# One attention layer reordered: rotary and shared-key head groups take turns

## The chip, the cores and the metric

The kernel runs on one core of one Trainium2 chip. The metric is the time of one execution in microseconds (us); lower is better. Three runs of the kernel before took 1016.63 to 1022.61 us, with a median of 1020.66.

The engines: PE multiplies matrices and writes to PSUM banks; DVE (vector) and ACT (activation) read those banks; POOL (GpSimd) works on SBUF only; SP issues all transfers (DMA).

## The reference, cut to what matters

The program is four transformer layers on 1024 tokens of width 256. Only layer 0 changes. It has two attentions on the same normalised input, added together: one of 16 heads with low-rank queries and keys and a rotary part of 64 rows per head (called MLA below), and one of 16 heads whose key and value are selected per token by a router (called shared below).

```python
    def _L0_attn_ref(x, Wqd, Wqu, Wqr, Wkvd, Wku, Wvu, Wkr, Wo):
        ...
        H, LAT, RD = (16, 64, 64)
        ...
        ql = x @ Wqd
        q = (ql @ Wqu)...
        qr = (ql @ Wqr)...
        qr = _apply_rope(qr, cos, sin)
        ckv = x @ Wkvd
        ...
        kr = _apply_rope((x @ Wkr)[:, None], cos, sin)[:, 0]
        scores = (jnp.einsum('bhtd,bhsd->bhts', q, k) + jnp.einsum('bhtd,bsd->bhts', qr, kr)) * scale
        ... # causal softmax, times v
    def _L0_ffn_ref(x, W_gate, W_qkv):
        ...
        k_shared = jnp.einsum('bth,bthd->btd', indicator, k)
        v_shared = jnp.einsum('bth,bthd->btd', gating_top1, v)
        att = jnp.einsum('bhqd,bkd->bhqk', q, k_shared) * (1.0 / math.sqrt(hd))
        ... # causal softmax, times v_shared
```

## The kernel before

Every engine runs its own program, written out by hand; semaphores tie them. The 16 heads of each attention are cut into groups of four (GH = 4). Layer 0 has eight groups: groups 0 to 3 are MLA, groups 4 to 7 are shared.

A group is worked off in eight steps kt, one per tile of 128 keys. In a step PE writes the transposed scores of the four heads into psA (L1549, L1550), ACT takes the exponential into Pr (L834, L839), POOL zeroes what the causal mask forbids (L709, `mask_exponentials`), and PE multiplies the exponentials of the step before by the values (L1587). An MLA score takes two f32 matmuls (128 rows of Kr2 and Qr2, 113 rows of Kr and Qr), a shared score one bf16 matmul. Since the scores stand transposed, the row maxima have to be known before the group starts. They come from 43 bf16 products per group (L1532, with masks L1534) into psD, which DVE reduces (L1088, 43 instructions). They are computed beside the group ahead: `max_window` and `beside` (L56, L63) say in which steps. At kt = 5 the maxima are transposed, copied by DVE into mrow, and SP carries them into row 112 of Qr (row 96 of Qs for a shared group): `maxima_row`, L505. The next group cannot start before that row has landed.

Ahead of the groups stands a prologue, ordered by the list PRE0 (L351). It computes the latents, the query and key rows without rotation (d_qn, d_kn), the rotary query rows of all 16 heads in eight pairs ("rope" 0 to 7: eight PE matmuls, four DVE products with cos and sin at L1067, a POOL sum at L679, an ACT copy at L874 and a subtraction for the low part), the router and the selected keys and values ("kv" 0 to 7), and the maxima of group 0. Query and key rows are stored to DRAM and loaded back in another layout by `load_group` (L477): three DMAs for the maxima (`stack_in`), then six for the scores (`rest_in`), 4.5 MB per MLA group. Groups 0 and 1 have a place each in Qr and Kr; the load of group i + 2 waits until group i has been scored. All go through SP's one queue.

Of the kernel before, what the change touches and what calls it, by code (L numbers as in the profile page):

```python
# [11 lines left out]
P = 128  # L12
# [43 lines left out]
def max_window(i, first, early):  # L56

    if early:
        return [(i - 1, kt) for kt in range(1, MAX_END)]
    return [(i - 2, kt) for kt in range(MAX_END, NT) if i - 2 >= first] + [(i - 1, kt) for kt in range(MAX_END)]  # L60


def beside(groups, i, kt):  # L63

    for g in (i + 1, i + 2):
        if g not in groups:
            continue
        window = max_window(g, groups[0], g <= NG)
# [16 lines left out]
def build(nc, ins, out):  # L85
    with ExitStack() as ctx:
# [61 lines left out]
        Qr2 = [over("WB", "Qr2a", [P, GH * T]), over("fT", "Qr2b", [P, GH * T])]  # L148
# [4 lines left out]
        lat_parts = over("Qs", "lat_parts", [P, T], 7 * T)  # L153
# [87 lines left out]
        def split_place(u):  # L241

            if u < 3:
                b = (0, w_qkv0_at, 3 * HALF)[u]
                return ((xnT[:, 0, :], xnT[:, 1, :], OT[:])[u],
                        WA[:, b:b + 3 * HALF].bitcast(BF16).rearrange("p (s t) -> p s t", s=3))
            b = 2560 * (u % 3)
            return (Pr[:, b:b + T],
                    Pr[:, b + T:b + 2560].bitcast(BF16).rearrange("p (s t) -> p s t", s=3))

# [18 lines left out]
        d_gk = dram("d_gk", (3, HD, T), BF16)  # L269
# [31 lines left out]
        def values(i, kt, h):  # L301
            return Vg[:, kt, :] if NG <= i < 2 * NG else Vh[:, kt, (h + GH * (i % NG)) * HV:(h + GH * (i % NG)) * HV + VW]
# [8 lines left out]
        def maxima_of(i):  # L311
# [5 lines left out]
            [("xnT0", DC), ("lat", 1), ("qn", 2), ("kn", 2), ("v0", 2), ("gq", 2), ("gk", 1)]  # L317
            + [(f"att{i}", A_GROUP) for i in GROUPS[0][:-1]] + [("oT0", DC), (f"att{2 * NG - 1}", A_GROUP)]
# [1634 lines left out]
```

## Time and profile before

| what | us |
|---|---|
| median of three runs | 1020.66 |
| the profiled execution, whole | 1021.14 |
| its span in the trace | 1019.4 |
| prologue, until the first score matmul of group 0 | 151.9 |
| groups 0 to 3 (MLA) | 195.7 |
| groups 4 to 7 (shared) | 139.7 |
| the rest, layers 1 to 3 | 532.1 |

The stages are cut where ACT takes the first exponentials of a group; the last line starts at the copy of group 7's output. Busy times of PE are of pipelined matmuls whose ends are modelled. PEclk is the clock granted to TensorE as a share of 2.4 GHz; over a long stretch it is a mean of its two levels, 1.0 (2.4 GHz) and 0.5 (1.2 GHz).

### The profile page before, as it was taken

How to read it: one execution, taken by the hardware profiler on the slowest of the kernel's cores; microseconds unless marked ns; L12 is line 12 of the kernel's file. 1: busy time of each engine (PE TensorE's matmuls, PEld its weight loads, DVE VectorE, ACT ScalarE, POOL GpSimd, SP SyncE). 2: the span in 40 equal slices, each digit the busy share in tenths (PEclk: the TensorE clock that was granted, in tenths of full speed). 3: DMA queues.
4: the chain of work that ended last, by engine and by line, in shares of the span. 5: the costliest groups of instructions: out<-in, count | busy, mean ns of one | idle time of the engine just before them, and what ended most of it. 6: DMA issues, size and time to landing. Idle time of an engine off the chain costs nothing.

```text
span 1019.4 us, 11908 instructions
## 1 busy us (share of the span) xinstructions
PE 872.7 (86%) x4799; PEld 507.4 (50%) x4799; DVE 566.7 (56%) x986; ACT 381.4 (37%) x470; POOL 222.6 (22%) x207
## 2 busy tenths in 40 slices
PE   4992969888799999989498998978999879969897
PEld 2451335444354433333246878543333248868676
DVE  4772665354457778741533355287777435954452
ACT  2520014425244546466244340213555664410331
POOL 2441422401010133311210100220111126710010
PEclk9976688989799999999587999876999979989799
DMA  5499546384815400000600000495300052000001
GB/s 169 179 206 194 206 74 125 60 128 113 136 30 122 58 7 1 1 2 1 215 0 1 1 0 32 134 169 76 52 2 1 1 188 70 1 1 1 1 1 42
DMA packets 33313, 71.32 MB, mean 70 GB/s; under 512 B 5637, under 2 KB 14413, under 8 KB 33254
## 3 DMA queue, kind: packets, MB, share of 16 engines
q1 hardware_dynamic: 33258, 70.56, 30.1%
q8 instruction: 38, 0.62, 0.3%
q14 instruction: 17, 0.14, 0.0%
HBM read 49.27 MB, written 18.48 MB: 66 GB/s over the span
## 4 chain that ended last, share of the span: by engine, by line
PE 66%; DVE 17%; ACT 5%; DMA 5%; issue 4%; POOL 1%; SPq 1%; DVEq 0%; ACTq 0%; POOLq 0%
PE psD L1468 11%; PE psA L1468 11%; PE psO L1587 10%; PE psO L1468 10%; PE psD L1532 8%; DVE mx L1088 8%; PE psA L1550 7%; PE psA L1549 3%; DMA Kr<-d_kn 2%; DVE hid_low L1382 2%; PE psD L1534 2%; ACT Pr L834 2%; PE psA L1500 1%; SPq L436 1%; POOL Pr L709 1%
## 5 line engine op out<-in xcount | busy, mean ns | idle before, releaser
L1088 DVE TENSOR_REDUCE mx<-psD 128x1 f32<-128x512 f32 (+3 forms) x416 | 258.0, 658 | 158.6 <-PE psD L1534 134.0
L834 ACT ACTIVATE Pr<-psA 128x1024 f32<-128x1024 f32 (+3 forms) x192 | 161.5, 865 | 169.0 <-PE psA L1550 168.4
L709 POOL TENSOR_SCALAR_AFFINE_SELECT Pr<-Pr 128x512 f32<-128x512 f32 x96 | 61.1, 636 | 405.2 <-ACT Pr L834 325.9
L839 ACT ACTIVATE Pr<-psA 128x1024 f32<-128x1024 f32 (+3 forms) x96 | 63.3, 702 | 60.3 <-PE psA L1550 59.9
L1587 PE MATMUL psO<-Pr,Vh 128*32 128x512 f32 (+3 forms) x768 | 81.5, 504 | 3.6 <-POOL Pr L709 3.0
L1532 PE MATMUL psD<-Kr,Qr 80*128 80x512 bf16 (+3 forms) x167 | 51.4, 360 | 36.7 <-issue 19.9
L1534 PE MATMUL psD<-maskq,identb 128*128 128x128 bf16 x349 | 72.5, 232 | 0.0
L1550 PE MATMUL psA<-Qr,Kr 113*128 113x512 f32 (+3 forms) x192 | 68.1, 360 | 0.0
L1532 PE MATMUL psD<-Kg,Qs 96*128 96x512 bf16 (+3 forms) x192 | 57.2, 331 | 5.4 <-DVE mx L1088 2.0
L1532 PE MATMUL psD<-Ks,Qs 96*128 96x512 bf16 (+3 forms) x166 | 54.8, 359 | 4.2 <-DVE mx L1088 3.3
L1532 PEld LDWEIGHTS psD<-Kr,Qr 80*128 80x128 bf16 x167 | 17.1, 105 | 78.0 <-issue 30.0
L1550 PE MATMUL psA<-Qs,Ks 97*128 97x512 bf16 (+3 forms) x192 | 45.8, 332 | 3.9 <-ACT Pr L834 3.3
L1550 PE MATMUL psA<-Qs,Kg 97*128 97x512 bf16 (+3 forms) x192 | 44.9, 326 | 3.8 <-ACT Pr L834 3.3
L1500 PE MATMUL psA<-identf,xn 128*128 128x128 f32 x96 | 21.4, 389 | 30.8 <-DVE xn L1056 30.4
L1532 PEld LDWEIGHTS psD<-Kg,Qs 96*128 96x128 bf16 x192 | 18.1, 97 | 54.9 <-DVE mx L1088 43.5
L1587 PE MATMUL psO<-Pr,Vg 128*32 128x512 f32 (+3 forms) x384 | 40.1, 497 | 2.0 <-POOL Pr L709 1.3
L1549 PE MATMUL psA<-Qr2a,Kr 128*128 128x512 f32 (+3 forms) x96 | 39.0, 420 | 3.0 <-issue 2.7
L1532 PEld LDWEIGHTS psD<-Ks,Qs 96*128 96x128 bf16 x166 | 16.7, 102 | 47.1 <-DVE mx L1088 41.4
L1550 PEld LDWEIGHTS psA<-Qr,Kr 113*128 113x128 f32 x192 | 38.2, 199 | 2.8
L1534 PEld LDWEIGHTS psD<-maskq,identb 128*128 128x128 bf16 x349 | 36.5, 105 | 4.5 <-issue 0.9
L1549 PE MATMUL psA<-Qr2b,Kr 128*128 128x512 f32 (+3 forms) x96 | 37.3, 401 | 0.7 <-ACT Pr L834 0.7
L1468 PE MATMUL psA<-xnT,WA 128*128 128x512 f32 x56 | 32.7, 749 | 2.2 <-ACT xnT L801 2.2
(392 smaller groups left out, 1712.0 us busy)
## 6 DMA issues: line engine op xcount, KB each, us to landing
d_qr<-Pr SPq DMA_DIRECT2D x16, 512.0 KB, 3.6
Qr<-d_qr SPq DMA_DIRECT2D x4, 1024.0 KB
Qr2a<-d_qr SPq DMA_DIRECT2D x4, 1024.0 KB, 24.7
Qr2b<-d_qr SPq DMA_DIRECT2D x4, 1024.0 KB, 20.1
Pr<-d_cb SPq DMA_DIRECT2D x8, 512.0 KB, 6.9
Qr<-d_qn SPq DMA_DIRECT2D x12, 256.0 KB, 13.9
Kr<-d_kn SPq DMA_DIRECT2D x12, 256.0 KB, 16.8
Qs<-d_gq SPq DMA_DIRECT2D x24, 128.0 KB
```

Of the source, the lines that this page charges most:

```text
L709: pool.affine_select(out=block_, in_=block_, pattern=[[0, GH], [1, P]], compare_op=ALU.is_ge, fill=0.0, base=0, channel_multiplier=-1).the ...
L834: act.activation(place[:, h, q0:T], src[:, q0:T], ACT.Exp, scale=score_scale(i)).then_inc(a_drained, 1)
L839: act.activation(place[:, h:h + 2, q0:T], src[:, :, q0 - HALF:HALF], ACT.Exp, scale=score_scale(i)).then_inc(a_drained, 1)
L1088: dve.tensor_reduce(mx[:, j, part, h0:h0 + nh], src, AX, ALU.max).then_inc(d_drained, 1)
L1382: dve.tensor_tensor(hid2_low[:, m - DC, :], slot(Qs, m - DC), hid2_high[:, m - DC, :], ALU.subtract).then_inc(hid2_split, 1)
L1468: op = pe.matmul(dst, lhsT, rhs, start=start and k == 0, stop=stop and k == len(terms) - 1)
L1500: op = pe.transpose(dst[:, tile_cols(j)], src[:, j, c * P:(c + 1) * P], identf[:])
L1532: op = pe.matmul(dst[:, k * w:(k + 1) * w], q, kk, start=True, stop=not diagonal)
L1534: op = pe.matmul(dst[:, (k + 1) * w - P:(k + 1) * w], identb[:], maskq[:], start=False, stop=True)
L1549: pe.matmul(out_, second[0], second[1](lo, (half + 1) * HALF), start=True, stop=False)
L1550: op = pe.matmul(out_, k, q(lo, (half + 1) * HALF), start=second is None, stop=not (diagonal and mask))
L1587: op = pe.matmul(psO[h * VW:(h + 1) * VW, lo:hi], values(i, kt, h), e, start=kt == 0, stop=kt == last_kt, tile_position=(0, h * VW), skip_ ...
```

## The change

Layer 0 is put in another order, on all engines. MLA groups are now 0, 2, 4 and 6, and shared groups 1, 3, 5 and 7. MLA groups have one place in Qr, Kr and Qr2 in turn, and are loaded in column halves (512 of 1024 columns): half 0 of group i + 2 once group i has been scored up to kt = 3, half 1 and the six rest loads, in halves too, once it is scored in full. Only rope 0 and 1 stay in the prologue; ropes 2 to 7 are computed at kt = 0 and kt = 2 of groups 0, 2 and 4. The shared keys reach Kg through a matmul and not through DRAM. The maxima of an MLA group all stand beside the shared group ahead of it; those of a shared group begin at kt = 5 of the shared group before and end in the MLA group. The output product's transposes move from the start of the last group to its kt = 3, Hadamard products of W_down from group 6 to group 7, and two sets of layer 1's weights are loaded earlier.

```diff
-def max_window(i, first, early):
-    if early:
-        return [(i - 1, kt) for kt in range(1, MAX_END)]
-    return [(i - 2, kt) for kt in range(MAX_END, NT) if i - 2 >= first] + [(i - 1, kt) for kt in range(MAX_END)]
+def is_mla(i):
+    return i < 2 * NG and i % 2 == 0
+ROPE_AT = {(0, 0): 2, (0, 2): 3, (2, 0): 4, (2, 2): 5, (4, 0): 6, (4, 2): 7}
+def max_window(i, first):
+    tail = [(i - 2, kt) for kt in range(MAX_END, NT) if i - 2 >= first and not is_mla(i)]
+    return tail + [(i - 1, kt) for kt in range(MAX_END)]
...
-        PRE0 = [("rope", 0), ("rope", 1), ("rope", 2), ("low", 0), ("low", 1), ("router",), ("rope", 3), ("kv", 0),
-                ("rope", 4), ("kv", 1), ("kv", 2), ("rope", 5), ("kv", 3)]
...
+        PRE0 = [("router",), ("lat",), ("kr",), ("nope", 0), ("rope", 0), ("rope", 1), ("nope", 2), ("gates",)]
+        PRE0 += [("kv", j) for j in range(NT)] + [("ksel",), ("gq", 0), ("v0",)]
+        among = {4: ("nope", 1), 10: ("nope", 3), 16: ("gk",), 24: ("gq", 1)}
...
+            def load_mla(i, half, places, s):
+                c = slice(half * HALF, (half + 1) * HALF)
+                for t, a, n, d in places:
+                    g = head_group(i) * GH * n
+                    load(t[a:a + n, 0:GH * T].bitcast(F32).rearrange("p (h t) -> p h t", h=GH)[:, :, c],
+                         d[g:g + GH * n, :].rearrange("(h d) t -> d h t", d=n)[:, :, c], s[half])
+            def load_high(i, half):
+                load_mla(i, half, ((Qr, 0, RD, d_qr[0]), (Qr, RD, HD, d_qn[0]), (Kr, RD, HD, d_kn[0])), mla_in)
+            def load_rest(i, half):
+                load_mla(i, half, ((Qr, RD + HD, HD, d_qn[0]), (Qr, RD + 2 * HD, HD, d_qn[1]),
+                                   (Kr, RD + HD, HD, d_kn[1]), (Kr, RD + 2 * HD, HD, d_kn[0]),
+                                   (Qr2, 0, RD, d_qr[0]), (Qr2, RD, RD, d_qr[1])), rest_in)
...
+            load_high(0, 0)
+            load_high(0, 1)
...
+            load_rest(0, 0)
+            load_rest(0, 1)
+            sp.wait_ge(split_done, 1)
+            load(d_gq[:, tile_cols(0), :].rearrange("s d t -> d s t"), split_place(0)[1], split_stored[0])
+            sp.wait_ge(split_stored[0], 16)
+            load_stack(1)
+            load_stack(3)
+            for u in (1, 3):
+                sp.wait_ge(nope_low, 2 + u // 2 + 1)
                 for part in range(2):
...
+                    nope_store(u, part)
             maxima_row(0)
...
             for i in GROUPS[0]:
...
+                if is_mla(i) and i < 2 * NG - 2:
+                    for p in (i + 2, i + 3):
+                        sp.wait_ge(rope_high, p + 1)
+                        rope_store(p, 0)
+                        sp.wait_ge(rope_low, p + 1)
+                        rope_store(p, 1)
+                    sp.wait_ge(rope_stored, 16 * 2 * (i + 4))
+                    sp.wait_ge(nope_stored, 16 * 8)
+                    sp.wait_ge(a_filled, scored(i, NT // 2 - 1))
+                    load_high(i + 2, 0)
                 if i + 1 in GROUPS[0]:
                     maxima_row(i + 1)
...
+                if is_mla(i) and i < 2 * NG - 2:
+                    sp.wait_ge(a_filled, A[f"att{i}"])
+                    load_high(i + 2, 1)
+                    load_rest(i + 2, 0)
+                    load_rest(i + 2, 1)
...
+                    if (i, kt) in ROPE_AT:
+                        rope_add(ROPE_AT[i, kt])
+                    if (i, kt - 1) in ROPE_AT:
+                        rope_rest(ROPE_AT[i, kt - 1])
...
+                        if (i, kt - 1) in ROPE_AT:
+                            rope_cut(ROPE_AT[i, kt - 1])
...
+                if is_mla(i) and (j, h0, part) == (NT // 2, 0, 0):
+                    pe.wait_ge(mla_in[1], 16 * MLA_DMAS * (i // 2 + 1))
...
+                        if (i, kt) in ROPE_AT:
+                            ahead = [("rope", ROPE_AT[i, kt], k) for k in range(4)] + ahead
```

Place one: PE's order early in the prologue, from the latents (the last operand of a product names its weights or its rows; lat_parts and wq_high, wq_low are a rotation's, xnT and WA the projections'). Before:

```order
L1468 MATMUL psD<-xnT,WA 128x512 x4
L1468 MATMUL psA<-OT,WA 128x512 x8
L1468 MATMUL psA<-WA,OT 128x256 x8
L1468 MATMUL psO<-lat_parts,wq_high 128x512
L1468 MATMUL psO<-lat_parts,wq_low 128x512
```

After:

```order
L1572 MATMUL psD<-WA,xnT 128x16 x16
L1572 MATMUL psA<-xnT,WA 128x512 x4
L1572 MATMUL psD<-xnT,WA 128x512 x2
L1572 MATMUL psO<-xnT,WA 128x512 x2
L1572 MATMUL psA<-OT,WA 128x512 x2
L1572 MATMUL psO<-lat_parts,wq_high 128x512
L1572 MATMUL psO<-lat_parts,wq_low 128x512
```

The router (128x16) comes first; one of the four unrotated row sets (psA<-OT,WA, two products each) stands ahead of the rotations where all four and the values stood before.

Place two: SP's queue from the first load of group 0 to the row of its maxima (Qr<-mrow). Qr, Kr and Qr2a or Qr_51 are the MLA places, Qs the shared one; d_ names are tensors in DRAM. Before:

```order
L436 DMA Qr2a<-d_qr 64x4x1024 x2
L436 DMA Kr<-xn 64x4x1024
L436 DMA d_qr<-Pr 128x1024 x12
L436 DMA Qr<-d_qr 64x4x1024
L436 DMA Qr<-d_qn 16x4x1024
L436 DMA Kr<-d_kn 16x4x1024
L436 DMA Qr<-mrow 1x32x128
```

After:

```order
L471 DMA d_qr<-Pr 128x1024 x2
L471 DMA Qr<-d_qn 16x4x512 x2
L471 DMA Kr<-d_kn 16x4x512 x2
L471 DMA Qr_51<-d_qr 64x4x512 x2
L471 DMA d_gq<-Pr 128x3x1024
L471 DMA Qs<-d_gq 16x4x1024 x12
L471 DMA d_qn<-WB 128x1024 x2
L471 DMA d_kn<-WB 128x1024
L471 DMA d_kn<-Pr 128x1024
L471 DMA Qr<-mrow 1x32x128
```

(The group of four rows from Qr<-d_qn to Qr_51<-d_qr stands twice in the program, once per half.) Between the last load of group 0 and its row of maxima SP now issues the first shared queries' store, two shared groups' loads and four stores of 512 KB.

Place three: SP's queue while group 0 is worked off and at its end. Before:

```order
L436 DMA Kg<-in_c_ones4b 1x1024
L436 DMA Qr<-mrow 1x32x128
L436 DMA Qr<-d_qr 64x4x1024
L436 DMA Qr<-d_qn 16x4x1024
L436 DMA Kr<-d_kn 16x4x1024
```

After:

```order
L471 DMA d_qr<-WB 128x1024 x2
L471 DMA d_qr<-xnT 128x1024
L471 DMA d_qr<-WB 128x1024
L471 DMA Qr<-d_qr 64x4x512
L471 DMA Qr<-d_qn 16x4x512
L471 DMA Kr<-d_kn 16x4x512
L471 DMA Qs<-mrowb 1x32x128
```

The next group's row of maxima went ahead of the next load; now it stands behind four stores of rotated rows and the first half of group 2.

## Rows read from the trace of the kernel before

**Rows 1.** Busy time by stage: stretch, length, PE, PEld, DVE, ACT, POOL, clock, DMA, GB/s.
```profile
0.00:80.00 80.00, 65.33 (x164) 32.22 (x164) 53.12 (x87) 24.29 (x31) 33.25 (x32) 0.91 0.68 182
80.00:99.70 19.70, 0.00 (x0) 0.02 (x1) 1.65 (x2) 0.88 (x1) 2.11 (x1) 0.58 1.02 200
99.70:151.90 52.20, 43.76 (x134) 18.99 (x134) 33.46 (x55) 5.06 (x5) 17.91 (x9) 0.73 0.48 144
151.90:196.00 44.10, 42.79 (x267) 24.52 (x268) 24.00 (x40) 19.14 (x24) 14.73 (x15) 0.93 0.44 79
196.00:302.00 106.00, 88.92 (x567) 49.12 (x566) 50.84 (x88) 39.89 (x50) 12.90 (x18) 0.92 0.59 106
302.00:347.60 45.60, 42.91 (x305) 23.99 (x304) 28.94 (x50) 19.95 (x25) 5.08 (x8) 1.00 0.40 84
347.60:381.60 34.00, 31.40 (x236) 12.37 (x235) 25.68 (x45) 19.40 (x25) 10.15 (x16) 1.00 0.32 45
381.60:455.50 73.90, 66.88 (x468) 25.83 (x466) 52.78 (x95) 40.54 (x53) 20.47 (x23) 1.00 0.00 1
455.50:487.30 31.80, 27.61 (x190) 12.05 (x190) 5.24 (x10) 19.97 (x28) 5.08 (x8) 1.00 0.08 23
487.30:1019.40 532.10, 463.15 (x2479) 308.33 (x2479) 291.04 (x517) 192.29 (x233) 100.87 (x80) 0.90 0.18 46
```

**Rows 2.** The chain that ended last, in time: start, us, what.
```profile
79.83 19.88 issue
195.56 11.93 DMA Kr<-d_kn
248.32 12.67 DMA Kr<-d_kn
302.77 5.32 DMA Qs<-d_gq
```

**Rows 3.** Timeline of PE in the prologue: start, us, instruction, count.
```profile
40.70 0.50 PE L1468 MATMUL psO<-lat_parts,wq_high 128*128 128x512 f32 x1
44.13 0.49 PE L1468 MATMUL psO<-lat_parts,wq_high 128*128 128x512 f32 x1
69.29 3.70 PE L1468 MATMUL psD<-WA,xnT 128*128 128x512 f32 x8
```

**Rows 4.** Timeline of DVE: maxima of a shared group, one step of kv.
```profile
348.48 5.98 DVE L1088 TENSOR_REDUCE mx<-psD 128x1 f32<-128x512 f32 x9 [0.15 <-PE psD L1534]
78.16 0.69 DVE L1245 TENSOR_TENSOR WA<-psO,sel 128x512 f32<-128x512 f32 x1 [0.80 <-PE psO L1468]
78.88 1.02 DVE L1247 TENSOR_REDUCE kvs<-WA 128x32 f32<-128x512 f32 x1
```

**Rows 5.** Timeline of POOL and ACT: parts of a rotation, and of the shared rotary key.
```profile
36.15 3.20 POOL L670 TENSOR_TENSOR xn<-xn 64x1024 fp32r<-64x1024 f32 x1
45.01 2.37 POOL L679 TENSOR_TENSOR Pr<-Pr 128x1024 f32<-128x1024 f32 x1 [5.66 <-DVE Pr L1067]
47.41 1.06 ACT L874 ACTIVATE Pr<-Pr 128x1024 fp32r<-128x1024 f32 x1 [5.39 <-POOL Pr L679]
```

**Rows 6.** Transfers: issuer, count, KB each, median us to landing.
```profile
d_qr<-Pr SPq DMA_DIRECT2D x16, 512.0 KB, 3.6
Kr<-xn SPq DMA_DIRECT2D x2, 1024.0 KB, 19.0
d_gk<-WA SPq DMA_DIRECT2D x1, 96.0 KB, 17.3
```

**Rows 7.** Busy time (columns of Rows 1) beside loads of MLA rows, and of shared rows.
```profile
200.00:210.00 10.00, 3.95 (x22) 3.26 (x21) 1.33 (x2) 2.98 (x4) 0.64 (x1) 0.80 1.05 131
260.00:270.00 10.00, 8.96 (x50) 4.67 (x50) 4.47 (x8) 1.83 (x2) 0.00 (x0) 0.63 1.03 146
305.00:310.00 5.00, 3.77 (x26) 2.84 (x27) 1.20 (x2) 3.41 (x4) 0.64 (x1) 1.00 1.07 139
```

**Rows 8.** Timeline of ACT in group 3: last exponential of kt 3, last, group 4's first.
```profile
332.68 0.71 ACT L834 ACTIVATE Pr<-psA 128x640 f32<-128x640 f32 x1 [1.88 <-PE psA L1550]
...
345.83 0.77 ACT L839 ACTIVATE Pr<-psA 128x256 f32<-128x256 f32 x2 [1.20 <-PE psA L1550]
347.61 1.94 ACT L834 ACTIVATE Pr<-psA 128x1024 f32<-128x1024 f32 x2 [1.01 <-PE psA L1550]
```

More of the change, by code:

```diff
@@ L458, in _ @@
             load(w_o0, tiles("Wo0"), w0b_in)
-            for u in range(4):
-                sp.wait_ge(low_ready, u + 1)
-                for part in range(2):
-                    load((d_qn, d_kn)[u // 2][part, tile_cols(u % 2), :], slot(Ks, 4 * part + u), mla_stored)
-            sp.wait_ge(mla_stored, 16 * 8)
-            sp.wait_ge(v_cleared, 3)
-            sp.wait_ge(kr_ready, 1)
-            def shared_key(first):
-                places = Kr[0:RD, first * T:(first + GH) * T].bitcast(F32).rearrange("p (h t) -> p h t", h=GH)
-                load(places, kr_t.unsqueeze(1).broadcast_to([RD, GH, T]), kr_in)
@@ L526, in _ @@
-            load_group(1, rest=(False,))
-            maxima_row(0)
-            load_group(1, rest=(True,))
-            sp.wait_ge(split_done, 1)
-            load(d_gk.rearrange("s d t -> d s t"), split_place(2)[1][0:HD], split_stored[2])
-            sp.wait_ge(split_stored[2], 16)
-            for r, part in enumerate(K_PARTS):
-                load(Kg[r * HD:(r + 1) * HD, :], d_gk[part], kg_in)
-            load(Kg[STACK:STACK + 1, :], ins["c_ones4b"][:, 0:T].bitcast(BF16), kg_in)
-            for i in GROUPS[0]:
+            sp.wait_ge(a_drained, A["nope0"])
@@ new lines, in _ @@
+            nope_store(0, 0)
+            sp.wait_ge(v_cleared, 3)
+            sp.wait_ge(kr_ready, 1)
+            load(Kr[0:RD, 0:GH * T].bitcast(F32).rearrange("p (h t) -> p h t", h=GH),
+                 kr_t.unsqueeze(1).broadcast_to([RD, GH, T]), kr_in)
+            load(Kr[MLA_ONE:MLA_ONE + 1, 0:GH * T].bitcast(F32), onesf[0:GH * T // P, :], kr_in)
+            for p in range(2):
+                sp.wait_ge(rope_high, p + 1)
+                rope_store(p, 0)
+            sp.wait_ge(a_drained, A["nope2"])
@@ new lines, in _ @@
+            nope_store(2, 0)
+            sp.wait_ge(rope_stored, 16 * 2)
+            sp.wait_ge(nope_stored, 16 * 2)
+            load_high(0, 0)
+            load_high(0, 1)
+            sp.wait_ge(kr_ready, 2)
+            load(Kr2[0:RD, :].bitcast(F32), kr, kr2_in)
+            load(Kr2[RD:2 * RD, :].bitcast(F32), kr_t, kr2_in)
+            for u in (0, 2):
+                sp.wait_ge(nope_low, u // 2 + 1)
+                nope_store(u, 1)
+            for p in range(2):
+                sp.wait_ge(rope_low, p + 1)
+                rope_store(p, 1)
@@ L822, in attention @@
                 for i in groups:
[L823 to L824 removed]
                     for kt in range(NT):
                         s = NT * i + kt
+                        if i == 2 * NG - 1 and kt == OUT0_KT:
+                            copy_units([fT[:, c, :] for c in range(DC)])
                         if s >= 2:
```

441 lines of the change are left out of this document (242 added, 199 removed).

## The prediction, on record before the change was run

> **What bounds the kernel now.** I read the busy times by stage first. In the groups PE is the engine without slack: 42.9 of 45.6 us in group 3, 31.4 of 34.0 in the first shared group; DVE has 28.9 and 25.7 there [rows 1]. The exceptions are gaps. The chain of waits shows them: 19.9 us of "issue" from 79.8 on, where PE stands before group 0's maxima, and 11.9 and 12.7 us behind the loads of groups 2 and 3, and 5.3 us (most of it covered) behind the shared queries [rows 2]. In the first gap PE does nothing, while the DMA engines are busy throughout, at 200 GB/s [rows 1]: it is a gap of transfers. Groups 1 and 2 together take 106 us where group 3 takes 45.6; in them TensorE's clock falls to 0.80 and 0.63 in the ten us around or behind a gap [rows 1, 7]. The reader is to see two kinds of cost: gaps in which transfers are late, and stretches in which PE's own work sets the pace. The change attacks the first and leaves the second nearly as it is.
>
> The profiled execution took 1021.1 us (span 1019.4), 0.5 above the median of 1020.7, so the sum is made against 1021.1.
>
> **The prologue, computing.** Up to the transposes and xnT nothing changes; PE is free at 18.8. Rates: a rotation takes PE 44.13 - 40.70 = 3.43 us; a kv step is half of 3.70, 1.85 us; in half clock these get up to twice as long [rows 3]. In the new order PE does the router, the latents, the shared rotary key, two of four unrotated sets and two rotations: about 5.8 + 3.4 to 6.8 + 3.5 + 3.7 + 6.9, and ends near 42 to 45. Eight kv steps follow, 14.8 us, of which I let three or four fall into half clock (the first 80 us have a mean clock of 0.91 [rows 1]): 63. DVE keeps up with 0.69 + 1.02 us each [rows 4]. Then the shared queries and the values, 7.3 us: 70. Now the 43 maxima. DVE takes 5.98 us for nine, 0.66 each [rows 4], 28.4 in all; nope 1 and 3, gk and gq 1 between them interrupt for some 3: 102. The row of maxima needs 3 more. If nothing else were late, group 0 would start at 105 instead of 151.9, 47 us sooner. What leaves is six rotations (20.6 us of PE), the 19.9 us gap, and half of the stall around it.
>
> **The prologue, transfers.** All is one queue, and what stands before the row of maxima in it must go first: the row d_gk landed 17.3 us after its issue, behind 3 MB of rests [rows 6], some 175 GB/s. The first stores wait for POOL. The shared key's sum, cast and subtraction (the last of them 3.2 us) precede two sums of 2.4 us, then ACT's cut of 1.1 [rows 5]; the fourth high store is issued near 51 and landed 3.6 us later [rows 6], 54.6. From there to the row of maxima the queue carries 1.5 MB of high loads, 0.5 of Kr2, four low stores (2), the rests (3), the shared queries' store (0.75), two shared groups (1.5) and four stores of unrotated rows (2): 11.25 MB. At the 200 GB/s of the stretch 80 to 99.7 [rows 1] that is 56 us, at the 146 beside a group's load [rows 7] 77 us. I take 180, between them and nearest to the first, since 4.75 MB of it are stores: 63 us, so 118, and 2 for the landing. **Group 0 starts at 120, not at 105**, and PE stands still for 15 us in front of it. The gain is 32 us; its ends are 46 (computing is the bound) and 20 (146 GB/s). The first maxima want only high half 0, which lands near 64, ahead of need: the gap at 79.8 goes, and a gap ahead of the row takes its place.
>
> **The groups.** I build each from the stage rows. Before they are 44.1, 106.0, 45.6, 34.0, 73.9 and 31.8: 335.4 us [rows 1].
> An MLA group without gaps: 45.6, less 1.3 of the wait for the shared queries and 1.5 for the seven maxima at its tail, 42.8. A maximum costs PE some 0.35 us; with 36 instead of 43 it is 40.3. A pair of rotations adds 2 x 3.43 = 6.9 us of PE; about 1 of it falls into slack of kt = 0, where four exponentials of a full row pace PE. DVE has room for the eight products. So group 0 takes 44.1 + 5.9 = 50.0, groups 2 and 4 take 46.2 each, group 6 39.3 (no rotation, the same 1 us of slack).
> A shared group gets 43 maxima in its first five steps where 36 stood, and 7 at its tail as before. There DVE is nearly full: seven more are 4.6 us, of which I let 1.6 fall into its pauses: 34.0 + 3.0 = 37.0, three times. The last group keeps its 31.8 and takes over the Hadamard products (4 us) and the transposes (1.9) from its predecessors, which are in the 73.9: 37.7.
> Sum without gaps: 50.0 + 92.4 + 39.3 + 111.0 + 37.7 = 330.4, so 5 us under before although 20.6 us of rotations were added: the old gaps of some 21 us pay for them.
>
> **New gaps at the end of an MLA group.** SP now issues, in this order: four stores of rotated rows, a wait until they have landed, the first half of group i + 2, and only then the row of maxima of group i + 1. The last low part exists only after the exponentials of kt = 3: ACT's cut 1.1, POOL's subtraction 2.4 [rows 5], store 0.5 + 3.6 [rows 6], three issues and 0.75 MB at 131 GB/s [rows 7] 1 + 5.7, and the small row behind it 2: 16.3 us after kt = 3 has ended. Group 3 before needs 347.6 - 333.4 = 14.2 us for what is left after that point [rows 8], and without its tail of maxima 12.7. So PE waits for about 4 us at the start of groups 1, 3 and 5, with nothing else to do: everything behind the wait on its queue is that group. Once it goes, the second half (8 us from its issue) comes about when the first of its maxima is due, at the end of kt = 0; I add nothing. Each wait costs clock as well: at a mean of 0.80 over ten us [rows 7], four us ran at half clock, so 2 us lost. Three times 6 is 18. The start of group 0 follows a longer stand than before (15 us against some 5), and after the stand at 80 to 99.7 the mean clock was 0.73 for 52 us [rows 1]; I add 3. For these three waits the bounds are 0 (the row lands in time) and 10 each.
>
> **The rest.** Earlier weights of layer 1 and the matmul in place of Kg's seven transfers were hidden before, and I count them as nothing: the loads end under the last group's output and normalisation, and Kg was in place long before the shared groups. If the cover were gone, it would be 1 or 2 us. POOL's four added operations per MLA group (9.5 us in all) fit between masks of 0.64 us that come every 5 us or so.
>
> **Sum.** Start -32; groups 330.4 + 18 + 3 = 351.4 against 335.4, +16; in all -16: **1005 us**.
>
> **Rivals.** (1) The queue runs faster than I take it, for example since stores move at twice the rate of loads, and rows of maxima land in time: start at 106 (-46), groups 330.4 (-5): 970 us. For it: the order was such that only the high half is needed first, and PE's work ends at 105. Against it: 11.25 MB in one line, and the gap at 79.8 to 99.7, which has the same cause. Chance 0.20.
> (2) Slower. The MLA loads in column halves, twice as many and with pieces of 2 KB instead of 4, run at two thirds of the old rate. Place: the 4.5 MB of group 0 and the half in front of each row of maxima. Price: 4.5 MB take 42 instead of 28 us, +14; three waits grow by 3 us and lose 1 of clock each, +12: 1031 us. It decides as soon as the halves run over 40% slower, where the 16 us are used up. For it: the many short pieces. Against it: shared queries have 2 KB pieces on 16 partitions already and run at 139 GB/s, no less than the 131 of MLA rows [rows 7]. Chance 0.13.
> The Trainium skill speaks against the change here ("SBUF — State Buffer", The DMA setup-cost knee): each transfer pays about 2 us that don't grow with its size, so one should send few large ones. By that rule, paid in line, nine more transfers per load would be 18 us ahead of group 0 and 6 at each of three ends, an estimate of 1041. The trace agrees only for a single transfer: twelve shared loads of 128 KB each would by that rule stay under 65 GB/s, and they run at 139, so the fixed part overlaps in a queue.
> (3) No gain: it does what it says, but the maxima in shared groups cost their full 4.6 us (+5), rotations find no slack (+4), and the waits are 6 us instead of 4 (+6): 1020. For it: DVE and PE wait for each other through two psD banks all through the groups. Against it: DVE is busy 25.7 of 34 us [rows 1]. Chance 0.14.
>
> **Numbers.** My forecast has 0.53. What a measurement of this kernel can tell from no change is 0.5%, 5 us. Faster than 1016: all of (1), 0.50 of the forecast's 0.53 and 0.03 of (3), 0.73. Within 5 us: most of (3) and the edge of the forecast, 0.14. Slower: (2), 0.13. The range goes from 980, between (1) and the forecast, to 1026, between the forecast and (2); my forecast alone spans 990 to 1019.
>
> **What would show it.** In the changed profile: PE's gap near 80 gone; the first score matmul between 106 and 132, with PE idle for 10 us or more before it and the DMA engines busy (right), or none (rival 1). Groups 2 and 4 at 46 us, shared groups at 37, the gap of 12 us behind Kr<-d_kn gone. At the start of groups 1, 3 and 5 a wait of 2 to 6 us whose last releaser is the transfer of mrowb. DVE nearly full in the first five steps of a shared group. The forecast is wrong if group 0 starts beyond 132, if a wait of over 10 us stands at a group's start, or if the stretch after layer 0 changes by more than 3 us.

## The result, and the profile after

The changed kernel takes 1024.7 us in the median of 20 runs (1017.6 to 1035.7), the one before 1018.6 (1015.8 to 1024.8); the ratio of the two is 1.0056, 95% interval 1.0035 to 1.0077. The change made the kernel slower by 0.6%, some 6 us. Some executions run longer as a whole at a lower granted clock (here two of the 20, 1033.3 and 1035.7 us), and ratios and readings of the profile below leave such executions out. The forecast was 1005 us; 1024.7 lies inside the range of 980 to 1026, but the sign, to which I gave 0.73, was wrong.

The profiled execution after spans 1021.5 us, 2.1 more than the one before. The other 4 us of the difference in medians aren't in these two profiles: the one before took 2.5 us more than its kernel's median, the one after 1.4 less. Busy time by stage, as in [rows 1]: stretch, length, PE, PEld, DVE, ACT, POOL, clock, DMA share, GB/s. The third stretch begins with group 0's scores, the next seven with the first exponential of groups 1 to 7, the last behind layer 0's last output copy.

```profile
0.00:80.00 80.00, 60.30 (x180) 31.78 (x180) 52.62 (x91) 20.13 (x26) 32.70 (x34) 0.95 0.59 155
80.00:114.40 34.40, 19.92 (x71) 7.96 (x69) 17.53 (x31) 3.98 (x4) 3.83 (x2) 0.65 0.94 202
114.40:174.00 59.60, 53.62 (x286) 28.56 (x287) 29.84 (x48) 20.91 (x26) 14.48 (x12) 0.84 0.23 62
174.00:216.50 42.50, 40.17 (x258) 16.08 (x255) 29.20 (x50) 19.76 (x25) 11.20 (x12) 0.84 0.51 101
216.50:268.30 51.80, 45.59 (x276) 24.19 (x276) 30.05 (x48) 21.52 (x27) 14.44 (x12) 0.98 0.33 80
268.30:311.20 42.90, 40.76 (x258) 16.18 (x255) 29.21 (x50) 19.76 (x26) 5.07 (x8) 0.83 0.48 83
311.20:363.10 51.90, 45.65 (x277) 24.29 (x277) 30.05 (x48) 21.57 (x28) 14.45 (x12) 0.99 0.33 79
363.10:417.20 54.10, 43.81 (x259) 16.75 (x257) 29.37 (x50) 19.81 (x25) 17.27 (x20) 0.76 0.52 103
417.20:461.90 44.70, 41.95 (x267) 22.36 (x265) 26.39 (x48) 19.94 (x25) 8.43 (x11) 1.00 0.07 22
461.90:495.70 33.80, 29.42 (x206) 13.65 (x204) 4.51 (x10) 22.12 (x29) 6.91 (x10) 1.00 0.09 25
495.70:1021.50 525.80, 460.19 (x2479) 307.21 (x2479) 287.11 (x517) 192.03 (x232) 99.32 (x78) 0.91 0.18 44
```

Group 0 starts 37.5 us sooner (114.4 against 151.9), but the eight groups take 381.3 instead of 335.4 us, and the rest 6.3 less than the 532.1 of [rows 1]: -37.5 + 45.9 - 6.3 = +2.1, the difference of the two spans. The shared groups 1, 3 and 5 show PE busy for 40 us and more, where the first one had 31.4 in 34.0 before, at a clock of 0.84, 0.83 and 0.76 instead of 1.00; and group 5 sticks out with 54.1.

Of the chain that ended last (start, length, what), the waits that answer to [rows 2]:

```profile
62.60 12.19 DMA d_qr<-Pr
...
81.56 15.09 DMA d_gq<-Pr
...
104.37 10.04 DMA Qr<-mrow
...
166.27 6.55 DMA Qs<-mrowb
...
260.95 6.19 DMA Qs<-mrowb
...
366.49 11.58 SPq L471
...
379.09 11.34 DMA WB<-in_W_upT
```

The first three are the prologue's one queue: PE's gap of 19.9 us at 79.8 has gone, and a stand of 11.6 us in front of group 0's scores has come. The waits of 12 us for `Kr<-d_kn` have turned into smaller ones for the row of maxima. The last two lines were in no forecast. SP hangs for 11.6 us at the issue of `su` (1.5 us before), behind 3 MB of rests, as I take it because the queue was full; the last of layer 1's weights lands at 390.4. POOL waits for them:

```profile
372.26 0.63 POOL L779 TENSOR_SCALAR_AFFINE_SELECT Pr<-Pr 128x512 f32<-128x512 f32 x1 [13.56 <-ACT Pr L908]
390.51 1.52 POOL L790 TENSOR_TENSOR fT<-WB 128x256 f32<-128x256 f32 x2 [17.62 <-DMA WB<-in_W_upT]
392.10 0.63 POOL L779 TENSOR_SCALAR_AFFINE_SELECT Pr<-Pr 128x512 f32<-128x512 f32 x1
```

This timeline of POOL (in brackets the idle time in front and what ended it) shows one mask at 372.3, then 17.6 us of nothing, then a butterfly, then the next mask. PE can't multiply values before the mask:

```profile
384.37 0.28 PE L1638 MATMUL psD<-Kr,Qr 80*128 80x256 bf16 x1
384.48 0.22 PE L1640 MATMUL psD<-maskq,identb 128*128 128x128 bf16 x1
392.79 1.51 PE L1693 MATMUL psO<-Pr,Vg 128*32 128x384 f32 x8 [8.09 <-POOL Pr L779]
```

Before, the same weights were issued at 306, in group 3; after, from 365.8 on, and POOL's program waits for them at kt = 0 of group 5.

### The profile page after: what moved, and what is told of

The parts are those of the page before. It is cut to its first block, busy times and chain, and to the rows that moved or that the text cites. A ratio compares the mean times of both kernels' runs of the same rounds, so it can differ in the third digit from the quotient of the medians.

```text
span 1021.5 us, 11944 instructions
## 1 busy us (share of the span) xinstructions
PE 881.4 (86%) x4799; PEld 509.0 (50%) x4799; DVE 565.9 (55%) x988; ACT 381.5 (37%) x470; POOL 228.1 (22%) x209
## 4 chain that ended last, share of the span: by engine, by line
PE 59%; DVE 17%; DMA 9%; ACT 5%; SPq 5%; POOL 3%; issue 2%; DVEq 0%; ACTq 0%; POOLq 0%
PE psD L1572 10%; PE psO L1693 9%; PE psA L1572 9%; PE psD L1638 8%; DVE mx L1180 7%; PE psO L1572 7%; PE psA L1656 7%; SPq L471 5%; PE psA L1655 3%; DVE hid_low L1486 2%; PE psD L1640 2%; DMA d_gq<-Pr 1%; PE psA L1604 1%; DMA Qs<-mrowb 1%; ACT Pr L908 1%
## 5 line engine op out<-in xcount | busy, mean ns | idle before, releaser
L1180 DVE TENSOR_REDUCE mx<-psD 128x1 f32<-128x512 f32 (+3 forms) x417 | 260.9, 658 | 143.1 <-PE psD L1640 101.9
L1655 PE MATMUL psA<-Qr,Kr 128*128 128x512 f32 (+3 forms) x192 | 76.7, 413 | 11.6 <-DMA Qr<-mrow 11.6
L1640 PE MATMUL psD<-maskq,identb 128*128 128x128 bf16 x348 | 75.8, 241 | 0.0
L1656 PE MATMUL psA<-Qs,Kg 97*128 97x512 bf16 (+3 forms) x192 | 53.9, 380 | 14.6 <-DMA Qs<-mrowb 12.1
L1638 PE MATMUL psD<-Kr,Qr 80*128 80x512 bf16 (+3 forms) x166 | 62.6, 416 | 3.5 <-DVE mx L1180 2.9
L1693 PE MATMUL psO<-Pr,Vg 128*32 128x512 f32 (+3 forms) x384 | 44.1, 541 | 9.4 <-POOL Pr L779 8.8
L1655 PEld LDWEIGHTS psA<-Qr,Kr 128*128 128x128 f32 x192 | 37.6, 196 | 24.2 <-issue 13.5
L1638 PEld LDWEIGHTS psD<-Kg,Qs 96*128 96x128 bf16 x192 | 18.2, 99 | 54.9 <-DVE mx L1180 36.7
L1638 PEld LDWEIGHTS psD<-Kr,Qr 80*128 80x128 bf16 x166 | 18.8, 114 | 53.6 <-DVE mx L1180 37.0
L1656 PEld LDWEIGHTS psA<-Qr,Kr 113*128 113x128 f32 x192 | 37.5, 195 | 2.3
L1656 PEld LDWEIGHTS psA<-Qs,Kg 97*128 97x128 bf16 x192 | 17.5, 107 | 33.5 <-DMA Qs<-mrowb 13.6
```

Of the source, the lines that this page charges most:

```text
L1180: dve.tensor_reduce(mx[:, j, part, h0:h0 + nh], src, AX, ALU.max).then_inc(d_drained, 1)
L1638: op = pe.matmul(dst[:, k * w:(k + 1) * w], q, kk, start=True, stop=not diagonal)
L1640: op = pe.matmul(dst[:, (k + 1) * w - P:(k + 1) * w], identb[:], maskq[:], start=False, stop=True)
L1655: pe.matmul(out_, second[0], second[1](lo, (half + 1) * HALF), start=True, stop=False)
L1656: op = pe.matmul(out_, k, q(lo, (half + 1) * HALF), start=second is None, stop=not (diagonal and mask))
L1693: op = pe.matmul(psO[h * VW:(h + 1) * VW, lo:hi], values(i, kt, h), e, start=kt == 0, stop=kt == last_kt, tile_position=(0, h * VW), skip_ ...
```

## Experiments

All are edits of the changed kernel. Times are medians; ratios are to the kernel before, measured in the same session, with the 95% interval (the changed kernel has 1.0056). "Groups" are lengths from first exponential to first exponential.

**1. The butterflies in group 6.**

```
-                    if i == 5:
+                    if i == 6:
                         if kt == 0:
                             pool.wait_ge(w1_in, 16 * N_W1)
```


> POOL's wait for layer 1's weights and its butterflies stand in group 6 instead of group 5. Theory A (the place of that wait costs a group): in group 5 POOL waits 17 us for the weights while masks of Pr are due, and PE stands from about 384 to 393; with the wait gone, 9 to 12 us go, and 2 to 5 more because TensorE's clock no longer falls behind the stand: 1010 to 1014, group 5 at 43 us like groups 1 and 3. Theory B (PE waits for something else there, such as loads of the same window, which moved 306 GB/s): group 5 keeps 50 us or more, time 1022 to 1025. If POOL is late in group 6 instead, that group grows by 5 or more.

1021.5 us, 1.002 [0.9995, 1.0044]. Group 5 shrank from 54.2 to 43.0, as theory A says, but only 3.9 us of it reached the end of layer 0, so the time missed theory A's 1010 to 1014. Group 6 grew from 44.7 to 50.3, the case that the last sentence of the expectation names. The chain shows where the rest went:

```profile
445.71 2.38 POOL fT L790
448.10 0.07 issue
448.17 2.35 POOL fT L790
450.51 0.04 issue
450.56 3.65 PE psD L1732 x4
```

The last butterflies, 2.4 us each, now end after group 6's last exponentials, and the Hadamard products wait. The wait had been moved, not removed.

**2. The second rotation at kt = 1.**

```
-ROPE_AT = {(0, 0): 2, (0, 2): 3, (2, 0): 4, (2, 2): 5, (4, 0): 6, (4, 2): 7}
+ROPE_AT = {(0, 0): 2, (0, 1): 3, (2, 0): 4, (2, 1): 5, (4, 0): 6, (4, 1): 7}
```


> The second rotation of a group is taken at kt = 1 instead of kt = 2, so that its low part exists one step sooner. Theory A (the wait at the starts of groups 1, 3 and 5 is for the row of maxima behind rope stores and the half load; the last low store decides): half loads issued 5 to 6 us sooner, the three waits of 4.6 us shrink below 1 us, and the 14 us at the lower clock behind each go too, 8 to 11 us each: 995 to 1003. Theory B (only the wait goes, the lower clock has another reason such as the change to shared groups): 3 x 4.6 = 14: 1011. Theory C (the half load waits for the exponentials of kt = 3 anyway and the row still stands behind it): 1020 or more.

1008.1 us, 0.9872 [0.9845, 0.9899]: 19 us less than the changed kernel. The time lies between theory A's 995 to 1003 and theory B's 1011, but the mechanism is theory A's, as the clock below shows. The half load of group 2 is issued at 156.9 instead of 164.3, the row of maxima finds the queue free, and PE doesn't wait. Busy time of four stretches inside and beside group 1:

```profile
160.00:168.00 8.00, 8.00 (x67) 4.87 (x64) 1.85 (x5) 3.56 (x7) 2.06 (x4) 1.00 0.35 62
168.00:176.00 8.00, 7.25 (x52) 2.92 (x53) 7.44 (x13) 5.76 (x7) 1.62 (x2) 1.00 1.02 164
176.00:184.00 8.00, 7.33 (x54) 2.92 (x50) 6.26 (x12) 3.55 (x5) 2.73 (x2) 1.00 1.08 179
184.00:205.00 21.00, 19.59 (x155) 7.81 (x156) 15.21 (x27) 9.99 (x15) 6.84 (x8) 1.00 0.45 105
```

The clock stays at 1.00, and groups 1 and 3 take 37.6 and 37.7 us instead of 42.5 and 42.9. Groups 0 to 4 are 19.6 us shorter in the profile (4.7, 4.9, 1.6, 5.2, 3.2). Group 5 is 1.8 longer (56.0): it begins sooner, but layer 1's weights don't come as much sooner, and what its start had won goes into POOL's wait.

**3. The row ahead of group 3's stack in the prologue.** (The four unrotated stores also move ahead of the wait for `split_stored`.)

```
             load_stack(1)
-            load_stack(3)
-            (nope stores 1 and 3)
             maxima_row(0)
+            load_stack(3)
```


> Prologue: unrotated low and high stores 1 and 3 are issued before the wait for the shared queries' store, and the stack of group 3 behind the row of maxima of group 0. Theory A (the transfers in front of the row hold group 0): the row is ready at 103.2 and landed at 114.4; it lands at 106 to 108, 6 to 8 us less, and up to 2 more if the clock falls less: 1015 to 1018. Theory B (group 3's stack or the stores are missed later, or computing is late anyway): 1022 to 1026.

1015.1 us, 0.996 [0.9935, 0.9986], 10 us less than the changed kernel. The row is issued at 101.4 and lands 4.4 us later instead of 10.0; the first exponential comes at 108.3 instead of 116.8. Theory A.

**4. The row ahead of the half load.**

```
-                    load_high(i + 2, 0)
                 if i + 1 in GROUPS[0]:
                     maxima_row(i + 1)
+                if is_mla(i) and i < 2 * NG - 2:
+                    load_high(i + 2, 0)
```


> In groups 0, 2 and 4 the row of maxima of the next group is issued before the half load of group i + 2, the rope stores stay in front of it. Theory A (the row's place in the queue is the cost): the wait of 4.6 us for mrowb goes at three starts, 14 us and part of the lower clock: 1000 to 1010. Theory B (the wait only moves: the first maxima of group i + 2, behind the first scores of group i + 1, need the half load, which lands as late as before): PE stands 3 to 5 us a step further on, at a maximum whose releaser is the load of Kr or Qr, and the time stays within 1020 to 1027.

1025.0 us, 1.0055 [1.0036, 1.0074]: no change, theory B. The wait has moved by one matmul group, to the first maximum of group 2:

```profile
173.97 0.23 PE L1639 MATMUL psD<-Kr,Qr 80*128 80x128 bf16 x1 [4.05 <-DMA Kr<-d_kn]
```

So the row's place in the queue is not the cause. What counts is how late the half load is issued, and by experiment 2 that hangs on the second rotation's low part. My forecast had named the queue order.

**5. PE busy in the waits.** 20 matmuls of 512 columns, not read by anyone, in front of the wait for the row in groups 1, 3 and 5.

```
+                    if is_shared(i) and i < 2 * NG - 1:
+                        filler(20)
                     pe.wait_ge(mrow_in, 16 * maxima_of(i))
```


> The changed kernel, with 20 matmuls of 512 columns whose results nobody reads put in front of PE's wait for the row of maxima at the starts of groups 1, 3 and 5 (some 4.4 us, about the length of that wait). The wait stays, only PE does something in it. Theory A (the stand itself costs 4.6 us, and the 14 us of half clock behind it 5 us more, because PE was idle): the clock stays at 1.00 in groups 1, 3 and 5, these take 38 to 39 us instead of 42.5 from first exponential to first exponential, and the kernel 1008 to 1013. Theory B (the clock falls for another reason than PE's stand, such as the loads that run there): groups 1 and 3 stay at 42 to 43 and the kernel at 1022 to 1027.

1019.5 us, 1.0003 [0.998, 1.0026]. The first exponential of group 1 comes only 1 us sooner, but the clock behind it is another. The changed kernel:

```profile
165.00:170.00 5.00, 3.25 (x32) 1.93 (x30) 0.00 (x0) 1.85 (x4) 1.36 (x3) 1.00 0.85 162
170.00:175.00 5.00, 2.13 (x12) 1.31 (x13) 0.20 (x1) 1.00 (x1) 0.00 (x0) 0.54 1.08 171
175.00:180.00 5.00, 4.76 (x26) 2.06 (x24) 3.33 (x6) 1.87 (x3) 0.00 (x0) 0.50 1.07 183
180.00:185.00 5.00, 5.00 (x21) 2.10 (x17) 3.21 (x6) 2.99 (x4) 1.62 (x2) 0.50 1.08 188
185.00:190.00 5.00, 4.82 (x31) 1.25 (x29) 3.18 (x6) 1.83 (x2) 0.00 (x0) 0.75 1.07 207
```

With the waits filled:

```profile
165.00:170.00 5.00, 5.00 (x39) 2.67 (x39) 0.00 (x0) 1.85 (x4) 1.27 (x2) 1.00 0.90 165
170.00:175.00 5.00, 4.64 (x33) 2.36 (x31) 1.54 (x3) 1.94 (x2) 0.00 (x0) 1.00 1.09 169
175.00:180.00 5.00, 4.77 (x33) 1.87 (x33) 4.76 (x9) 2.88 (x4) 0.76 (x2) 1.00 1.07 163
180.00:190.00 10.00, 9.15 (x63) 3.40 (x62) 8.12 (x15) 5.05 (x7) 3.58 (x3) 1.00 1.07 187
```

Same loads, same GB/s, clock 1.00 (2.4 GHz) instead of 0.50 (1.2 GHz) for some 15 us. Groups 1 and 3 take 37.7 and 37.6 us, as without any wait: the lower clock alone costs 5 us per start. That is theory A for the groups. The total came out between its 1008 to 1013 and theory B's 1022 to 1027, since groups 2 and 4 took 55.0 and 54.9 in the profiled execution instead of 51.9; there the clock fell to 0.50 for 7 us from 235 on, behind PE waits of 0.8 and 0.3 us for `otmp` and a rotation's product (see the last section).

**6. Half the rotations' work on PE** (in the kernel of experiment 2; rotations 4 to 7 without the product with the weights' low part).

```
-                product(d_unit(), [(wq_high...), (wq_low...)]).then_inc(d_filled, 1)
+                product(d_unit(), terms if p < 4 else terms[:1]).then_inc(d_filled, 1)
```


> As the kernel with rotations at kt = 0 and 1, but rotations 4 to 7 leave out their second product (the low part of the weights), so that PE does 4 instead of 8 matmuls of 0.43 us in each; the heads of groups 2 to 7's rotated queries lack that part. Groups 2 and 4 take 50.2 and 48.7 us there, group 6 without rotations 39.9. Theory A (a rotation costs PE's own time, 3.4 us, and what it adds comes from PE being the engine without slack): each group falls by 3.4 (2 x 1.7), the kernel by 7. Theory B (it costs the turns with DVE through psD's two banks, and PE's matmuls lie beside them): each group falls by less than 1.5, the kernel by 0 to 3.

998.7 us, 0.9791 [0.9761, 0.9821], 8 us under experiment 2. Groups 2 and 4 fell from 50.2 and 48.7 to 46.5 and 44.8, by 3.7 and 3.9 each. Theory A: a rotation in a group costs at least what PE needs for it (half of a pair is 3.4 us of PE).

**7. The butterflies from kt = 4 of group 5 to kt = 2 of group 6.**

```
-                    if i == 5:
-                        if kt == 0:
+                    k = NT * (i - 5) + kt - 4
+                    if 0 <= k < 8:
+                        if k == 0:
                             pool.wait_ge(w1_in, 16 * N_W1)
-                        for step in steps_1[2 * kt:2 * kt + 2]:
+                        for step in steps_1[2 * k:2 * k + 2]:
```


> The changed kernel with the butterflies alone moved, from kt = 4 of group 5 to kt = 2 of group 6. Theory A (the three costs add): group 5 takes 43 us instead of 54, no wait for fT in front of the last group; 1024.7 - 11 - 1 to 5 for the clock behind the stand and the last group's start: 1008 to 1013. Theory B (the weights land only at 391, after kt = 4 of group 5 is due, so that part of the wait stays until the loads in front are earlier, too): group 5 at 47 or more, 1015 to 1019, and the three help each other.

1015.7 us, 0.9965 [0.9942, 0.9988], 9 us under the changed kernel. Group 5 takes 43.1 us, the weights are there in time, and the last group starts without a wait; theory A's mechanism. The median missed its bound by 3 us and lies in theory B's 1015 to 1019; in the profiled execution group 4 took 55.8 instead of 51.9, in the manner of experiment 5.

**8. Edits 2, 3 and 7 together.**

> The second rotation at kt = 1, the prologue's row ahead of group 3's stack, and the butterflies from kt = 4 of group 5 to kt = 2 of group 6. Theory A (three separate costs, which add): start of group 0 at 108 instead of 115 (-7), no wait at three starts (-18), and POOL's 15 us stand of group 5 gone without one at the last group's start (-11 to -15): against the changed kernel's 1024.7, 985 to 990. Theory B (POOL's wait comes back in the butterflies, as when they stood in group 6 alone, where 10.7 us won in group 5 left 3.9): 994 to 998.

982.3 us, 0.9616 [0.9587, 0.9645], 3 us below theory A's 985 to 990: 39 us faster than the kernel before, 45 than the changed one. By themselves the edits are worth 18.8, 9.8 and 9.3 (differences of the ratios times 1020), 38 in sum. The other 7 lie, as far as single profiled executions show it, in group 5: edit 2 alone made it 1.8 us longer (54.2 to 56.0), but where POOL no longer waits there, it makes it 5.1 shorter, from 43.1 (experiment 7) to 38.0 (the kernel of the three with a filled prologue, below); 6.9 between these.

**9 to 12. More of the prologue.** Three copies of DVE (the expectations say four) as `tensor_tensor`, one of them shown, alone and with the three; the gates moved between latents and shared key; and unread matmuls behind the last 25 of group 0's maxima and behind its transposition.

```
-                link(dve.tensor_copy(sel[:, :, 0, :], ind))
+                link(dve.tensor_tensor(sel[:, :, 0, :], ind, ind, ALU.max))
```


> The changed kernel with those four copies alone made by tensor_tensor. Theory A (VectorE's row was ready at 103.2, but the queue let it go only at 104.4 and land at 114.4: transfers hold group 0): the row is ready some 7 us sooner and group 0 starts where it did: 1023 to 1026. Theory B (VectorE's lateness holds group 0): 1016 to 1019.

> As the three together, and four copies of VectorE in the prologue (sel from rt, two casts and copies of the shared key and value) are made by tensor_tensor with max of a value with itself. Theory A (these copies wait for a port that GpSimd's tensor_tensor holds, and a tensor_tensor of VectorE doesn't): the 5.8 us copy takes below 0.5, the kv steps start 5 us sooner, and the row of maxima is ready at 94 to 97 instead of 103; group 0 then starts 3 to 7 us sooner, as far as transfers allow: 980 to 985. Theory B (VectorE is slowed whatever the form, or the row then waits for the rests and the shared queries' store): within 2 us of the three together.

```
-        PRE0 = [("router",), ("lat",), ("kr",), ("nope", 0), ("rope", 0), ("rope", 1), ("nope", 2), ("gates",)]
+        PRE0 = [("router",), ("lat",), ("gates",), ("kr",), ("nope", 0), ("rope", 0), ("rope", 1), ("nope", 2)]
```


> The three together, with the four operations of the gates (the last two write sel) moved from behind the rotations to just behind the latents, where GpSimd does nothing. Theory A (VectorE's 5.8 us copy waits until GpSimd's unbroken row of operations ends, whatever its own form): it takes 0.2 to 0.3 us there, the kv steps start 4 to 5 us sooner, the row of maxima is ready near 99.5, and group 0 starts 2 to 4 us sooner: 978 to 981. Theory B (the copy is slow by its form or its data): 5.8 us also there, 982 to 984.

```
                     maxima_unit(0, j, h0, nh, w, part)
+                    if MAX_UNITS.index(item[2]) >= 18:
+                        filler(1)
             maxima_transpose(0, GH)
+            filler(20)
```


> The three together, with one unread matmul behind each of the last 25 of group 0's maxima and 20 while its row is under way. Theory A (group 0's first 15 us run at half clock because PE stood or idled before it): the clock is 1.00 from group 0's start, which takes 49 to 51 us instead of 53 to 59, and the kernel 974 to 978 against 982. Theory B (PE at half clock can't keep up with one matmul more per maximum, and the row is later): start of group 0 at 112 or later, kernel at 982 to 988.

> The three together with both: early gates and filled prologue. If both count: 971 to 975. If filling slows the maxima: 980 to 985. If group 0's start is set by transfers near 105: 976 to 979.

Copies alone: 1023.5 us, 1.0027 [1.0003, 1.005], and with the three 982.6, 0.9626 [0.9598, 0.9655]: nothing that can be told apart, and for another reason than I wrote, since the new form was as slow (5.9 us, rows below). So whether DVE or the transfers hold group 0 was not tested by it. The kernel with both early gates and filled prologue does show it, for itself: its row of maxima was ready at 91.9, but SP issued it only at 98.2, behind the wait for the shared queries' store, and PE stood 10.3 us for it until 106.5. There the transfers hold group 0. Early gates with the three: 980.2, 0.9616 [0.9575, 0.9657]; there the copy took 0.23 us as in theory A, yet in this execution the first kv step still began at 52.9, now behind 6.0 us of waiting for PE. Filled prologue with the three: 980.0, 0.9628 [0.959, 0.9666]; both: 981.5, 0.9638 [0.9608, 0.9668]. In the profiled execution of the filled one group 0 took 47.8 us against 51.0 and 51.2 in two unfilled ones, but 52.5 in the one with both, and the medians don't confirm a gain: whether group 0's start can be kept at full clock this way stays open. None of these is better than the three together by more than the measurement can tell.

## Why the prediction was wrong

Set beside the forecast, with each wait put where it falls, the times in us are (forecast, measured): start of group 0 120, 114.4; group 0 57, 59.6; shared groups 1 and 3 39 each, 42.5 and 42.9; groups 2 and 4 50.2 each, 51.8 and 51.9; group 5 39, 54.1; group 6 39.3, 44.7; the last group 37.7, 33.8; the rest 532.1, 525.8. The forecast's 351.4 us of groups became 381.3, +29.9, against -5.6 at the start and -6.3 in the rest; these three, +18.0, are the miss of the span (1003.4 forecast, 1021.5 measured). Of the 29.9, 11 to 12 are POOL's wait in group 5 and 9 the clock at three starts, both below; the other 9 lie in group 0 (2.6), groups 2 and 4 (1.6 and 1.7), the last two (1.5) and some 0.7 in each of groups 1, 3 and 5.

- **Prologue, computing: right in the number, in part by luck.** DVE's row of maxima was ready at 103.2, forecast 105, although a copy took 5.8 us instead of 0.2, which no term held. In the kernel with early gates, where the copy is fast, the row was ready at 98.8; so my other terms were too long by about as much.
- **Prologue, transfers: right in kind, the start forecast 5.6 us too late.** The gap at 79.8 went, PE stood 11.6 us ahead of group 0 (forecast 15) with the queue at 202 GB/s, above the 180 I took. The truth was near the upper of my two bounds, the 200 GB/s. The 11.25 MB of the sum were also too few: `Kr<-xn` is 1024 KB and not 0.5 MB.
- **Groups without gaps: near, 1.9 us short for groups 2 and 4.** 46.2 us were forecast; 51.8 less a wait of 3.7 is 48.1. I had let 1 us of the two rotations fall into slack, but by experiment 6 half of their work on PE is worth 3.7 and 3.9 us, more than its own 3.4: they found no slack. A shared group: 37.0 forecast, 37.6 measured (experiment 2). The last group and group 6 together are 78.5 against 77.0: the Hadamard products fell into the one, not the other.
- **Waits at the starts of groups 1, 3 and 5: right in place and length, wrong in the clock.** PE waits 12.1 us in three for `mrowb`, 3.7 to 4.6 each (forecast 4). But I gave the clock 2 us each, taken as four us of a ten-us mean of [rows 7]; it takes 5 (experiment 5), so this term was mis-sized by 3. The rows I used ended too early: they held the stand and its first microseconds, not the whole stretch at 1.2 GHz behind it. Three times 3 is 9 us. And I named the row's place in the queue as the reason; experiment 4 refutes that, experiment 2 shows the lateness of the last low part.
- **Group 0 at the cold clock: near.** +3 forecast; 59.6 against 57.
- **"Earlier weights of layer 1 ... were hidden before, and I count them as nothing": the step that failed.** I looked at the loads that end under the last output, and not at those of `w1_in`. The section on the change calls both sets earlier, and that is wrong for this one: it is issued at 365.8, where it was issued at 306. The change put it behind the rests of group 6 in SP's queue, and POOL waits for it in group 5 with masks queued behind that wait. I had written that POOL's additions fit between the masks, from their durations, and never asked what POOL's program waits for. It cost group 5 54.1 against 42.5 to 42.9 of its like: 11 to 12 us, where I had priced lost cover at 1 or 2. Experiment 7 takes this wait away and nothing else, and the kernel gets 9 us faster, from 1.0056 to 0.9965: with this term at nothing, as forecast, the sign would have been right, by little. A wait of over 10 us was on my list of what would refute the forecast, but I looked for it at a group's start.
- **The rest: 6.3 us less, where I said nothing changes.** 3.9 of it lie in the last normalisation of layer 0 (below), and come from the other set of weights, which is in truth earlier: the term that I had put at nothing was off in both directions.

Of the rivals, (3) with 1020 us was the nearest total, but mostly not for its reasons: only the rotations without slack are borne out. The maxima cost about what I took and the waits were 4 us, and it held neither the clock at 5 us nor POOL. Rival (2), slow halves, is refuted: beside the half-width MLA loads the queue moves 162 to 207 GB/s (experiment 5's windows), more than the 131 and 146 of [rows 7]. The rule of the Trainium skill ("SBUF — State Buffer", The DMA setup-cost knee), by which I had estimated 1041 for nine more transfers in line, isn't what happened either: by the trace the halves cost no rate.

## What to carry to other kernels

When a change moves the issue of a load, look up every engine that waits on its semaphore and what is queued behind that wait: POOL's masks stood behind weights whose products PE wanted only 80 us later, and this alone undid nearly a third of the 37.5 us that the earlier start had gained. Price a stand of PE as its own length plus the stretch at half clock behind it, read to the point where the clock is back (it doesn't always fall, as the last section shows), and look for the last producer of the late transfer before you reorder the queue. The three small edits of experiment 8 turn 6 us lost into 39 won.

## What the runs showed of the hardware

**Some DVE operations stand while GpSimd works.** The copy `sel<-rt` took 0.23 us in the kernel before, with GpSimd idle. In the changed kernel, and in the form of a tensor_tensor (the kernel of the three and DVE's copies), it took:

```profile
45.85 5.84 DVE L1327 COPY sel<-rt 128x128 f32<-128x128 f32 x1
```
```profile
44.01 5.89 DVE L1328 TENSOR_TENSOR sel<-rt 128x128 f32<-128x128 f32 x1
```

GpSimd's operations beside the second:

```profile
42.78 4.66 POOL L734 TENSOR_TENSOR Pr<-Pr 128x1024 f32<-128x1024 f32 x2
47.39 2.36 POOL L744 TENSOR_TENSOR Qs<-Qs 128x1024 fp32r<-128x1024 f32 x1
```

DVE's operation ends 0.15 us after the third of them, where GpSimd makes a pause of 0.7 us. Not every DVE operation waits: those that read PSUM ran beside GpSimd's undisturbed (0.69 us each), and so did a reduction (0.28) and a reciprocal (0.20) in SBUF right in front of the copy. The Trainium skill ("SBUF — State Buffer", SBUF: two separate sides) says that a DVE operation in a two-port mode or with two SBUF inputs and a GpSimd operation exclude each other for the length of the one that came first; the trace agrees as to which operations wait, but here the copy waited for three instructions of GpSimd, not one. The same in layer 0's last normalisation explains most of what the rest gained: in the kernel before, a 128x8 operation met GpSimd's two subtractions, 4.6 us from 495.1 on. In the changed kernel, whose weights for them are issued at 456.8 instead of 483.4, they run from 497.6 to 502.4 and are over when that operation comes. Before and after:

```profile
495.16 2.33 DVE L1053 TENSOR_SCALAR ln<-ln 128x8 f32<-128x8 f32 x1
497.52 0.20 DVE L1054 RECIPROCAL ln<-ln 128x8 f32<-128x8 f32 x1
497.76 4.41 DVE L1056 TENSOR_SCALAR xn<-x,mv,ln 128x256 f32<-128x256 f32 x8
```
```profile
503.47 0.17 DVE L1140 TENSOR_SCALAR ln<-ln 128x8 f32<-128x8 f32 x1
503.68 0.20 DVE L1141 RECIPROCAL ln<-ln 128x8 f32<-128x8 f32 x1
503.92 2.67 DVE L1143 TENSOR_SCALAR xn<-x,mv,ln 128x256 f32<-128x256 f32 x8
```

Of 6.3 us, 3.9 are these. The 128x8 operation ended at 497.49, in the middle of the two subtractions, which left no pause between them. So in this trace DVE got its turn after one instruction, in the prologue after three; what decides that stays open.

**Behind the same short waits the clock fell in one execution and stayed in another.** In the kernel with filled waits PE stood 0.8 us and 0.3 us in front of two rotation products at 232 to 234, since DVE's sum `x<-x,otmp` had taken 1.99 instead of 0.42 us beside GpSimd's addition. Windows of 2 us:

```profile
232.00:234.00 2.00, 0.99 (x3) 0.37 (x2) 1.86 (x6) 0.81 (x1) 0.00 (x0) 1.00 0.65 262
234.00:236.00 2.00, 1.99 (x10) 0.53 (x10) 1.25 (x2) 0.00 (x0) 0.00 (x0) 0.76 0.00 0
236.00:238.00 2.00, 2.00 (x8) 0.89 (x4) 0.26 (x1) 0.00 (x0) 0.00 (x0) 0.50 0.00 0
...
242.00:244.00 2.00, 1.79 (x12) 1.11 (x11) 1.75 (x3) 0.81 (x1) 0.00 (x0) 1.00 0.00 0
```

The clock fell to 1.2 GHz and came back 7 us later, with PE busy throughout. In the changed kernel the same sum took the same 1.99 us, and PE stood 0.76 and 0.27 us in front of the same products at 238 to 240, but the clock stayed:

```profile
238.00:240.00 2.00, 0.97 (x4) 0.41 (x3) 1.89 (x5) 0.81 (x1) 0.00 (x0) 1.00 0.65 262
240.00:242.00 2.00, 2.00 (x11) 0.67 (x11) 1.19 (x2) 0.00 (x0) 0.00 (x0) 1.00 0.00 0
```

So such a stand alone doesn't decide it, and no run here shows what does. Groups 2 and 4 take 52 to 57 us from execution to execution with the second rotation at kt = 2, the long ones with such a fall of the clock in the three that I read (groups 2 and 4 of experiment 5, group 4 of experiment 7).
